# Second stage of a two-layer graph kernel: the four matmuls that share a message piece are put side by side

## The reference, cut to what matters

```python
h = relu(layernorm(x))                                  # x: 8192 x 128, adj: 8192 x 8192 of 0 and 1
Wh = h @ W
e = leaky_relu(Wh @ a1 + (Wh @ a2).T)
att = softmax(where(adj > 0, e, -9e15))
x = x + relu(att @ Wh)                                  # first layer
h = relu(layernorm(x))
node = h @ W1                                           # 8192 x 16
msg = einsum('nk,nkf->nf', node, einsum('nc,kcf->nkf', h, W2))
x = x + relu(adj @ msg + node @ b)                      # second layer
```

## Time and profile before

| what | value |
|---|---|
| median of three runs | 1878.35 us |
| the profiled execution | 1875.03 us |
| its span, first to last instruction | 1873.4 us |
| second stage, first to last of its matmuls | 1355.7 to 1863.4 us of the span |
| PE, DVE, ACT, POOL busy, share of the span | 97%, 65%, 71%, 38% |
| mean granted TensorE clock | 0.991 of full |

### The profile page before, as it was taken

The page is one execution under the profiler, slowest core; times in us unless marked ns, Lnnn a source line. Parts: engine busy times, 40 slices in busy tenths (PEclk is TensorE's granted clock), DMA queues, the critical chain, the costliest instruction groups (busy, mean ns, idle before and its releaser), DMA issues.

```text
span 1873.4 us, 38193 instructions
## 1 busy us (share of the span) xinstructions
PE 1814.5 (97%) x13300; PEld 1586.9 (85%) x13300; DVE 1210.6 (65%) x1511; ACT 1330.3 (71%) x2144; POOL 715.7 (38%) x530
## 2 busy tenths in 40 slices
PE   4699999999999999999999999999999999999998
PEld 4599989889889988988988888898777788888886
DVE  6666677767767767767776776776656543443434
ACT  4666787878778787887788778878455655555554
POOL 0300056546545655654655565565535400000000
PEclk9799999999999999999999999999999999999999
DMA  9378967776776776777777677673753344445330
GB/s 332 153 303 327 347 249 276 289 282 259 289 290 250 295 287 256 287 286 273 268 289 277 264 292 278 252 297 152 302 204 144 137 164 160 155 159 204 151 158 22
DMA packets 105811, 452.23 MB, mean 241 GB/s; under 512 B 6736, under 2 KB 15136, under 8 KB 87968
## 3 DMA queue, kind: packets, MB, share of 16 engines
q1 hardware_dynamic: 86720, 356.53, 51.0%
q10 hardware_dynamic: 12208, 75.62, 9.9%
q0 software_dynamic: 6832, 19.41, 2.8%
HBM read 364.46 MB, written 87.07 MB: 241 GB/s over the span
## 4 chain that ended last, share of the span: by engine, by line
PE 90%; DVE 4%; ACT 3%; issue 2%; DMA 1%; POOL 1%; ACTq 0%; DVEq 0%; POOLq 0%
PE ot_ps L796 45%; PE mt_ps L840 13%; PE ot_ps L840 13%; PE hw_ps L760 11%; PE mt_ps L728 5%; ACT wh_mask L505 1%; DVE p_sb L961 1%; PE h_ps L755 1%; PE ot_ps L708 1%; DVE att L937 1%; ACT prod L571 1%; DVE p_sb L887 0%; DVE keep L942 0%; DMA keep_d<-keep 0%; PE h_ps L767 0%
## 5 line engine op out<-in xcount | busy, mean ns | idle before, releaser
L796 PE MATMUL ot_ps<-wh_mask,p_sb 128*128 (+1 forms) x8192 | 980.2, 277 | 6.4 <-DVE p_sb L961 6.4
L961 DVE SCALAR_TENSOR_TENSOR p_sb<-zb,qcol,mt 128x1024 f32<-128x1024 uint8 (+1 forms) x512 | 781.0, 1556 | 262.6 <-ACT mt L517 211.6
L796 PEld LDWEIGHTS ot_ps<-wh_mask,p_sb 128*128 128x128 f32 x8192 | 941.3, 192 | 9.0 <-issue 5.9
L378 POOL TENSOR_TENSOR prod<-prod 128x1024 f32<-128x1024 f32 (+2 forms) x192 | 409.2, 2131 | 516.5 <-ACT prod L571 499.3
L505 ACT ACTIVATE wh_mask<-adj_sb 128x2048 uint8<-128x2048 f32 x256 | 492.8, 1928 | 1.1 <-ACT mt L517 1.1
L632 ACT ACTIVATE mask<-adj_sb 128x1024 fp32r<-128x1024 uint8 x240 | 255.4, 1065 | 176.4 <-PE ot_ps L840 176.4
L517 ACT ACTIVATE mt<-mt_ps 128x1024 uint16<-128x1024 uint16 x256 | 267.6, 1046 | 151.8 <-PE mt_ps L728 150.5
L999 DVE CAST mask<-adj_sb 128x1024 fp32r<-128x1024 uint8 x272 | 202.2, 750 | 249.6 <-PE mt_ps L840 247.8
L571 ACT ACTIVATE prod<-hw_ps,node 128x128 f32<-128x128 f32 x1024 | 278.8, 385 | 92.1 <-PE hw_ps L760 92.1
L840 PE MATMUL mt_ps<-mask,msgs 128*128 128x512 f32 x1024 | 282.8, 398 | 4.3 <-issue 3.3
L840 PE MATMUL ot_ps<-mask,msgs 128*128 128x512 f32 x1024 | 275.5, 391 | 0.7
(11 more groups left out here) (110 smaller groups left out, 592.2 us busy)
## 6 DMA issues: line engine op xcount, KB each, us to landing
adj_sb<-in_adj_dram SPq DMA_DIRECT2D x128, 2048.0 KB, 8.0
maskT_d<-mt ACTq DMA_DIRECT2D x64, 1024.0 KB, 5.2
adj_sb<-maskT_d SPq DMA_DIRECT2D x32, 2048.0 KB, 7.5
keep_d<-keep POOLq DMA_DIRECT2D x64, 128.0 KB, 5.9
p_sb<-keep_d SPq DMA_DIRECT2D x4, 2048.0 KB, 12.0
msg_d<-msg POOLq DMA_DIRECT2D x56, 128.0 KB, 5.9
msgs<-msg_d SPq DMA_DIRECT2D x7, 1024.0 KB, 8.7
wh_mask<-in_x_dram SPq DMA_DIRECT2D x8, 512.0 KB, 7.3
```

Of the source, the lines that this page charges most:

```text
L378: pool.tensor_tensor(prod[:, 0:n, :], prod[:, 0:n, :], prod[:, n:2 * n, :], ALU.add)\
L796: ins = pe.matmul(ot_ps[h][:, (t - t0) * ROW:(t - t0 + 1) * ROW], p_sb[:, r, t * P:(t + 1) * P], rows, start=False, stop=end and t == t1 - 1)
L961: dve.scalar_tensor_tensor(p_sb[:, r, :], zbf[:, bass.ds((ib % 2) * BLK, BLK)], qcol[:, bass.ds(tile + b_, 1)], mtb[:, p, k, :, b_], ALU.m ...
```

## The change

The order of the loops over `ib` and `c` is exchanged. For each piece `c` the four matmuls (two `ib`, two `h`) now follow each other. The waits for the converted mask of (`t`, `ib`) stay ahead of the first matmul that reads it, and the signal `conv_used[r][ib]` stays on the last one. The eight matmuls of a step are the same ones with the same operands; the order in which a step's contributions reach each bank is unchanged.

```diff
-                    for ib in range(2):
-                        if t == 0 and not first:
-                            pe.wait_ge(y_act, 2 * (ii - 1) + ib + 1)
-                            pe.wait_ge(y_dve, 2 * (ii - 1) + ib + 1)
-                        if first and on_dve(first, t, ib):
-                            pe.wait_ge(conv_dve, dve_count(True, t, ib))
...
-                        pe.sem_inc(past_pe, 1)
-                        for c in range(2):
+                    for c in range(2):
+                        for ib in range(2):
+                            if c == 0:
+                                if t == 0 and not first:
+                                    pe.wait_ge(y_act, 2 * (ii - 1) + ib + 1)
+                                    pe.wait_ge(y_dve, 2 * (ii - 1) + ib + 1)
+                                if first and on_dve(first, t, ib):
+                                    pe.wait_ge(conv_dve, dve_count(True, t, ib))
...
+                                pe.sem_inc(past_pe, 1)
                             for h in range(2):
                                 ins = pe.matmul(acc_ps[2 * ib + h][:, :], msgs[:, t, c, :],
                                                 mask32[:, r, ib, h * HB:(h + 1) * HB],
                                                 start=t == 0 and c == 0, stop=t == NT - 1 and c == 1)
-                        ins.then_inc(conv_used[r][ib], 1)
+                            if c == 1:
+                                ins.then_inc(conv_used[r][ib], 1)
```

More of the change, by code:

```diff
@@ L824, in gather @@
                         pe.wait_ge(msgs_in[s], 16)
-                    for ib in range(2):
-                        if t == 0 and not first:
-                            pe.wait_ge(y_act, 2 * (ii - 1) + ib + 1)
-                            pe.wait_ge(y_dve, 2 * (ii - 1) + ib + 1)
-                        if first and on_dve(first, t, ib):
-                            pe.wait_ge(conv_dve, dve_count(True, t, ib))
[L831 to L836, removed]
-                        pe.sem_inc(past_pe, 1)
-                        for c in range(2):
+                    for c in range(2):
[6 more added lines that the diff above has]
+                                    pe.wait_ge(conv_dve, dve_count(True, t, ib))
+                                elif first:
+                                    pe.wait_ge(conv_act, act_count(True, t, ib))
+                                elif on_dve(first, t, ib):
+                                    pe.wait_ge(conv_dve, first_dve + (ii - 1) * NT + t + 1)
+                                else:
+                                    pe.wait_ge(conv_act, first_act + (ii - 1) * NT + t + 1)
+                                pe.sem_inc(past_pe, 1)
                             for h in range(2):
```

## The result

| | before | after |
|---|---|---|
| median (6 runs each) | 1878.73 us | 1886.62 us |
| lowest to highest | 1877.72 to 1879.83 | 1882.22 to 1888.12 |
| ratio, 95% interval | | 1.0039 [1.0026, 1.0052] |
| span of the profiled execution | 1873.4 | 1884.9 |

The change makes the kernel 7.9 us slower, 0.4%. The prediction said slower, by 5.0 us, with a range of 1878.5 to 1885.8, and the measured median lies above it. The interval of the ratio is 4.9 to 9.8 us, so the times alone would just allow 5.0.

What follows compares the result with a forecast made beforehand. A pass was taken to be bound by PE's matmul rate. Loads 0, first pass 3.3, boundaries 1.5 and end 0.15 gave 5.0 us, added to 1878.35 for 1883.3 us, range 1878.5 to 1885.8.

Steps and rivals of the forecast that it cites:

- Loads: Line 840: all 2048 weight loads remain, gain 0; dropping at least 1024 would be worth 0 to 13.7 us.
- Steady steps: About 60 steps of each pass: masks needed 0.453 us earlier, buffers freed 0.453 later, slack 0.80 and 1.16 left, nothing added.
- The two more matmuls behind the released wait: First pass, once per seven steps: six matmuls instead of four before the next step, 0.42 us each, seven times, 2.95 us.
- the wait of step 13: First pass, t = 13: PE's mask wait moves forward, it stands 0.31 us, absorbed by a later wait ending at 1393.93.
- The round's DVE chain: First pass: DVE makes xn, then two conversions; the PE wait behind them still ends at 1393.93, nothing added.
- Step 55: First pass: the only one of eight similar mask waits with no later wait to absorb it, so it pays 0.37 us.
- Boundaries and end: Banks ready later, second wanted sooner: 0.5 us at each of three pass boundaries, 1.5 us, plus 0.15 at the end.
- Rival 3: Waits bite in every step: 0.08 us more in half of 240 steady steps, 9.6 us more, 1892.9 us; chance 0.08.
- rival 2: Loads are shared: four neighbours with one piece need one load, 13.7 us off the forecast, 1869.6 us; chance 0.04.
- rival 1: First-pass delays are hidden; only boundaries and end pay, 0.9 to 2.5 us, 1879.2 to 1880.8 us; chance 0.27.

Runs made afterwards that it cites:

- alternating kernel: Kernel before with its inner loops over piece and half exchanged, so successive matmuls never share a message piece: ratio to before 0.9999 [0.9991, 1.0008].
- Old order in step 5 alone: Changed kernel with the old matmul order in first-pass steps with t % 7 = 5 only: 1883.32 us, ratio to before 1.0031 [1.0019, 1.0043].
- masks on ACT: Changed kernel with first-pass masks of t % 7 = 1, ib = 1 converted by ACT instead of DVE: 1880.74 us, ratio to before 1.0012.
- small first addition: Changed kernel with POOL's first addition of each of the last eight tiles cut from eight heads to one: a round 17.03 us, single run.

## Why the prediction was wrong

The direction and both places were right; the size failed in one step.

- *Loads.* Right. 2048 loads before and after, and the alternating kernel shows that sharing brings nothing. The value 0 stood nearer than the 13.7 of the bound. The rule of the Trainium skill ("TensorE: Matmul & The Clock Gate", Part 2, step 1), that one load can serve many matmuls, stays unshown here: the program as built has a load for every matmul.
- *Steady steps.* Right: 1.81 us, slack 0.95 and 1.00 for ACT's mask, no wait.
- *The two more matmuls behind the released wait.* Right: predicted 0.42 a round. Old order in step 5 alone leaves 17.45, which is 0.39 above before's 17.06, and the way from the released matmul to the next step is 1.49 for 1.09 to 1.14. That the wait of step 13 is absorbed in step 15 was right too; only where that wait is gone (masks on ACT, small first addition) does step 13 set the round.
- *The round's DVE chain.* This is the step that failed: its end was taken as fixed and its change put at nothing. The prediction said that PE arrives late "at a wait that ends at 1393.93 all the same". The end of that wait is not fixed. DVE's conversion for step 14 starts two matmuls later, because its buffer comes free at matmul 6 of step 12; that was worked out for the steady steps only, as slack, and not followed into the first pass. There it falls onto the start of POOL's first addition, which grows by 0.44; xn ends with that addition, and behind xn stand the conversions that PE waits for. 0.44 x 7 = 3.1 us was not in the sum. It was read as if a DVE instruction had a duration of its own; the 1.36 us of xn in the earlier trace rows was already for the most part a wait (0.34 without POOL beside it), and the prediction took it for work.
- *Step 55.* Predicted 0.37, measured 0.40 (2.21 for 1.81).
- *Boundaries and end.* Predicted 1.5 + 0.15, measured 1.7 + 0.14; undoing them gives back 1.8.

The sum as measured: 7 x 0.39 + 7 x 0.44 + 0.4 + 1.8 = 8.0, beside 8.2 of the profiles and 7.9 of the medians. The bounds of the terms held 4.2 at most for the first pass, so the range ended too low: it took in the bounds of the terms that it named, and none for a DVE chain that moves. Rival 3, waits in every step, would have given 14.6 and is refuted by the steady steps; rival 2, shared loads, by the 2048 loads and the alternating kernel; rival 1, hidden delays, by the first pass.

## What to carry to other kernels

Reordering matmuls so that neighbours share a stationary operand gains nothing where each matmul brings its own load; count the loads in the trace before, where neighbours already share. An order that reads a double buffer earlier and frees it later takes its price from every place where the slack is thin, so look for the shortest slack in the kernel and not for the usual one. When an instruction's start is moved on an engine, look at what then runs beside it, and where one instruction is several times longer than its size explains, find what it ends with before its end is taken as fixed.

## What the runs showed of the hardware

- A DVE tensor_scalar of 128x128 f32 lasted 1.36, 1.80 or 1.24 us, each time ending 0.08 to 0.09 us behind the POOL addition that ran when it started, and 0.34 where POOL ran nothing. POOL's 128x1024 addition took 2.35 us with no DVE conversion at its start, 2.48 with one over its first 0.22 us and 2.92 with one over its first 0.67; the conversions kept their 0.69 to 0.70. The Trainium skill has the rule ("SBUF — State Buffer", Who interferes with whom): VectorE and GpSimd share one pair of ports, and when VectorE runs in a mode that uses both its port pairs, whoever starts first holds the shared pair for its whole instruction while the other is blocked. The trace agrees in both directions, with the numbers above; which mode of DVE's instructions takes the pair no run here shows.
- A 32-column load took 109 ns for 188 with 128 columns, and matmuls of 512 columns with it stood 231 ns apart for 227.
- The number of matmuls at the low clock at the start of the second stage differed from profile to profile: 6 to 8 in seven of the eleven, 13 or 14 in four, worth some 1.2 us, more than some of the effects looked for. PE had stood idle 3.3 to 3.8 us ahead of the stage in all eleven.
